# A fused attention and expert-routing kernel: eight pieces for the first layer's weights, halves for the second, and a shorter last add

## What is computed

```python
def _L0_ffn_ref(x, controller, f1, bias, f2):      # x: normalised, (4, 1024, 512)
    grouped = x.reshape(B, g, t, d)                # g = 32 groups of t = 32 tokens
    logits = einsum('bgtd,des->bgtes', grouped, controller) + tie     # e = 32, s = 4
    perm = (logits == max(logits, axis=t))         # each of 128 (e, s) picks one token of a group
    dispatched = einsum('bgtd,bgtes->bgesd', grouped, perm)
    inner = relu(einsum('bgesd,desf->bgesf', dispatched, f1) + bias)  # f = 32
    intermediate = einsum('bgesf,esfd->bgesd', inner, f2)
    return einsum('bgesd,bgtes->bgtd', intermediate, perm)
...
x = x + attention(layernorm(x), ctx)
x = x + ffn(layernorm(x))
```

## Time and profile before

| | before |
|---|---|
| median of 3 runs | 1225.07 us (1223.57 to 1226.09) |
| the profiled execution | 1224.32 us |
| its span from first to last instruction | 1222.6 us |
| mean granted clock of TensorE | 0.979 of full speed |
| TensorE, VectorE, ScalarE, GpSimd busy | 94%, 70%, 49%, 44% of the span |
| DMA | 223.42 MB, mean 183 GB/s |

### The profile page before, as it was taken

One profiled execution on the slowest core, in us unless ns is written; L12 is line 12 of the kernel. 1 busy time (PEld: TensorE's weight loads), 2 busy tenths in 40 slices (PEclk: granted clock), 3 DMA queues, 4 the chain that ended last, 5 costly groups with the idle time before them and its releaser, 6 DMA issues. The chain is left out here.

```text
span 1222.6 us, 28711 instructions
## 1 busy us (share of the span) xinstructions
PE 1145.3 (94%) x11328; PEld 788.3 (64%) x11328; DVE 860.9 (70%) x2200; ACT 599.5 (49%) x1110; POOL 536.2 (44%) x740
## 2 busy tenths in 40 slices
PE   7999999999999999999999999998899997879886
PEld 6787888886555555555555555553578886767664
DVE  7765677763777777777777777774478886755765
ACT  4222222214565566556556655656244443437774
POOL 1000000012777666777766677777566640001344
PEclk9999999999999999999999999999989998989998
DMA  8978877885566444556644456622588874863555
GB/s 288 349 257 295 275 270 262 291 254 157 131 138 139 102 101 105 118 132 139 139 100 103 101 117 136 139 73 69 211 295 265 261 254 125 297 230 87 166 167 166
DMA packets 169733, 223.42 MB, mean 183 GB/s; under 512 B 9728, under 2 KB 97280, under 8 KB 168576
## 3 DMA queue, kind: packets, MB, share of 16 engines
q1 hardware_dynamic: 169600, 221.61, 61.6%
HBM read 143.69 MB, written 77.63 MB: 181 GB/s over the span
## 5 line engine op out<-in xcount | busy, mean ns | idle before, releaser
L1072 ACT ACTIVATE p_t<-p_bank 128x512 f32<-128x512 f32 (+1 forms) x608 | 304.7, 578 | 185.0 <-PE p_bank L1180 182.1
L936 DVE CUSTOM_DVE_ANT_0 tried<-p_bank,ban 128x128 bf16<-128x128 f32 (+3 forms) x512 | 237.2, 485 | 69.9 <-PE p_bank L1159 66.7
L1159 PE MATMUL p_bank<-k_stack,q_stack 96*128 96x512 f32 (+3 forms) x768 | 278.2, 377 | 4.9 <-DVE mx_ab L939 0.8
L1180 PE MATMUL p_bank<-q_stack,k_stack 97*128 97x512 f32 (+3 forms) x768 | 260.0, 359 | 11.2 <-ACT p_t L1072 9.8
L939 DVE TENSOR_REDUCE mx_ab<-p_bank 128x1 f32<-128x512 f32 x256 | 176.1, 688 | 57.2 <-PE p_bank L1159 55.6
L1159 PEld LDWEIGHTS p_bank<-k_stack,q_stack 96*128 96x128 f32 x768 | 144.3, 189 | 103.0 <-issue 39.8
L1180 PEld LDWEIGHTS p_bank<-q_stack,k_stack 97*128 97x128 f32 x768 | 145.6, 191 | 46.4 <-ACT p_t L1072 29.9
L821 POOL TENSOR_SCALAR_AFFINE_SELECT p_t<-p_t 128x128 f32<-128x128 f32 (+2 forms) x288 | 103.7, 362 | 160.2 <-ACT p_t L1072 153.5
L1199 PE MATMUL p_bank<-p_t,v_tile 128*32 128x512 f32 (+3 forms) x1536 | 164.7, 497 | 0.0
L832 POOL TENSOR_TENSOR p_sum<-p_sum,p_t 128x512 f32<-128x512 f32 x128 | 160.1, 1287 | 0.0
L1448 POOL TENSOR_TENSOR kept_o_sum<-kept_o_sum,kept_x_in 128x512 f32<-128x512 f32 x32 | 40.9, 1281 | 179.1 <-ACT kept_o_sum L1476 178.4
(11 more groups left out here) (132 smaller groups left out, 2079.3 us busy)
## 6 DMA issues: line engine op xcount, KB each, us to landing
q_stack<-q_hi SPq DMA_DIRECT2D x64, 256.0 KB, 6.8
k_stack<-k_hi SPq DMA_DIRECT2D x30, 512.0 KB, 9.6
kept_f<-in_f SPq DMA_DIRECT2D x5, 2048.0 KB, 10.7
x_in<-in_x SPq DMA_DIRECT2D x8, 1024.0 KB, 9.9
x_t<-in_x_t SPq DMA_DIRECT2D x8, 1024.0 KB, 9.0
k_hi<-k_hi_s SPq DMA_DIRECT2D x8, 1024.0 KB, 5.9
k_lo<-k_lo_s SPq DMA_DIRECT2D x8, 1024.0 KB, 7.8
v_rows<-v_out SPq DMA_DIRECT2D x8, 1024.0 KB, 7.7
```

The lines of the kernel that those rows point to most:

```text
L936: dve.tensor_tensor_reduce(scrap, got, ban0[:] if i == 0 else ban[:, CH - w:CH], 1.0, -3e38, ALU.add, ALU.max, to[:, col:col + 1]).then_in ...
L1072: act.activation(pt[:, k % SLOTS_P, u * m:(u + 1) * m, 0:w], bank[:, SB + n % SR, 0:m * w].rearrange("p (m w) -> p m w", m=m), ACT.Exp, sc ...
L1159: pe.matmul(bank[:, to, 0:w], qs[it % SLOTS][0:R, i * P // CH, h, i * P % CH:i * P % CH + P], ks[it % SLOTS][0:R, h, t0:t0 + w], start=Tru ...
L1180: mm = pe.matmul(bank[:, SB + n % SR, h % m * w:(h % m + 1) * w], ks[slot][0:R + 1, h, j * P:(j + 1) * P], qs[slot][0:R + 1, sh, h, CH - w ...
```

## The change

It has three parts. (1) The two loads of f1 quarters 0 and 1 (2 MB each, rows of 16 KB) after step 1 become eight loads of 512 KB (rows of 4 KB), after steps 2, 5, 8, ..., 23. The bias stays after step 1. (2) In the second layer the half of the columns becomes the outer loop and the batch the inner one. Each of the four f2 pieces is loaded in two parts: columns 0 to 255 (1 MB, rows of 1 KB) where the whole piece was loaded, columns 256 to 511 after the pick loads. Unit 4, the first of the second half, waits for them. (3) The last two of the 32 sums are no longer copied by ScalarE and added to by GpSimd; VectorE adds x2 to them directly from PSUM.

```diff
+    F1_PARTS = 4
...
             if s == 1:
-                sp.dma_start(keep.f1[:, 0], f1_src[0]).then_inc(f1_early, 16)
-                sp.dma_start(keep.f1[:, 1], f1_src[1]).then_inc(f1_early, 16)
                 sp.dma_start(keep.bias[:], a.bias_col).then_inc(f1_early, 16)
+            if s % 3 == 2 and s // 3 < 2 * F1_PARTS:
+                k, part = divmod(s // 3, F1_PARTS)
+                cols = slice(part * NE * F // F1_PARTS, (part + 1) * NE * F // F1_PARTS)
+                sp.dma_start(keep.f1[:, k, cols], f1_src[k, :, cols]).then_inc(f1_early, 16)
...
-        sp.wait_ge(f1_early, 48)
+        sp.wait_ge(f1_early, 16 + 2 * F1_PARTS * 16)
...
-    SUMS = [(h * CHUNKS + ch, b * 2 + w) for b in range(B) for h in range(HALVES) for ch in range(CHUNKS) for w in range(2)]
+    LAST = 2
+    SUMS = [(h * CHUNKS + ch, b * 2 + w) for h in range(HALVES) for b in range(B) for ch in range(CHUNKS) for w in range(2)]
...
-                    sp.dma_start(f2[i], f2_src[i]).then_inc(f2_in[i], 16)
+                    sp.dma_start(f2[i][:, :, 0:DH], f2_src[i][:, :, 0:DH]).then_inc(f2_in[0][i], 16)
...
                 def store(v):
-                    sp.wait_ge(added, v + 1)
+                    if v < len(SUMS) - LAST:
+                        sp.wait_ge(added, v + 1)
+                    else:
+                        sp.wait_ge(added_last, v - len(SUMS) + LAST + 1)
...
+                for i in range(len(f2)):
+                    sp.dma_start(f2[i][:, :, DH:D], f2_src[i][:, :, DH:D]).then_inc(f2_in[1][i], 16)
...
             def _(pool):
-                for v in range(len(SUMS)):
+                for v in range(len(SUMS) - LAST):
...
-                for w in range(2):
-                    keep_sum(len(SUMS) - 2 + w)
...
+                for v in range(len(SUMS) - LAST, len(SUMS)):
+                    dve.wait_ge(x_in[v % XR], 16 * (v // XR + 1))
+                    dve.wait_ge(stored[v % SR], 16 * (v // SR))
+                    dve.wait_ge(summed, v + 1)
+                    dve.tensor_tensor(o_sum[:, v % SR].rearrange("p n d -> p (n d)"), bank[:, SUM + v % 2],
+                                      x2[:, v % XR].rearrange("p n d -> p (n d)"), ALU.add).then_inc(added_last, 1)
...
-                    b, h, mp, qp = u // HALVES, u % HALVES, pair // 2, pair % 2
+                    b, h, mp, qp = u % B, u // B, pair // 2, pair % 2
                     n = u * PAIRS + pair
+                    if b == 0:
+                        pe.wait_ge(f2_in[h][mp], 16)
                     if u == 0:
-                        pe.wait_ge(f2_in[mp], 16)
                         pe.wait_ge(active, mp * 2 + 2)
```

More of the change, by code:

```diff
@@ L1367, in experts @@
         inner_done = sem("inner_done")
-        f2_in = [sem(f"f2_in{i}") for i in range(len(f2))]
+        f2_in = [[sem(f"f2_in{h}_{i}") for i in range(len(f2))] for h in range(HALVES)]
         pick_in = sem("pick_in")
@@ L1378, in experts @@
         added = sem("added")
+        added_last = sem("added_last")
         xn_src = m.xn.rearrange("(i p) (k d) -> k p i d", p=P, d=P)
```

## The result

The changed kernel takes 1217.59 us (median of 6 runs, 1214.3 to 1218.76), the kernel before 1223.52 in the same comparison. The medians are 5.9 us apart; the ratio of the means (1216.99 and 1223.98) is 0.9943, 95% interval 0.9927 to 0.9959, which is 7.0 us or 0.6% faster, and ratios are of means from here on. In a second comparison it was 0.9941 (0.9918 to 0.9965). The forecast was 1209.5 with a range of 1203 to 1216: the direction was right, and the gain is a little less than half of what was forecast.

What follows compares the result with a forecast made beforehand. TensorE, busy for 94% of the span, was taken as the bound. 10.0 (routing) + 4.0 (expert stage, net) + 1.3 (end) = 15.3 us off 1224.32 gives 1209.0; with the median 0.75 higher, 1209.5, range 1203 to 1216.

Steps and rivals of the forecast that it cites:

- The eight pieces: Routing stage: splitting the two 2 MB f1 loads removes TensorE's hole near 881 to 888, 10.0 us gained.
- upper bound of 15.8 us: Routing stage: the most the pieces could cost, 4.19 MB at 266 GB/s wholly in the tiles' way; 0 was taken.
- (c): Rival, routing stage: the pieces are hidden only in part, costing 3 us of TensorE; 1212.5 us, chance 12%.
- (d): Rival, routing stage: the hole at 881 is the stage's start-up, not the 4 MB, and stays; 1219.5 us, chance 6%.
- (e): Rival, slower: small rows make DMA the bound; routing loses 15.8 us, the halves cost 4; 1233 us, chance 5%.
- The last two sums: End of the kernel: VectorE adds from PSUM instead of ScalarE copying and GpSimd adding, 1.3 us gained.
- The wait for x2: End of the kernel: x2 rows landing after 4.4 us instead of 3.4 would take half the gain, 0.6 to 1.3.
- Stalls of layer one: Expert stage: three large TensorE instruction stalls, 6.70 us in all, shrink to 1.06 each with f2 halved, 3.5 us gained.
- the clock: Expert stage: TensorE's slow clock behind the last stall may go; a third of 3.0 us taken, 1.0 us gained.
- The comparison with the stop at 1038: Layer one: this stop, 1.06 us beside 512-byte rows only, was taken as what each of three large stalls would cost.
- What the second halves add: Start of layer two, 1107 to 1121: second halves of f2 cost 0.5 us, since ScalarE sets the pace; bounds 0 to 4.
- Rival (a): Expert stage: instruction stalls do not depend on what else is queued, and stay; 1214 us, chance 17%.

Runs made afterwards that it cites:

- e5: The changed kernel without loading the second halves of f2; all units use the first halves: 1212.27 us, ratio 0.9903 to the kernel before.
- e1: The changed kernel with each f2 piece loaded whole again (2 MB), no second halves behind the picks: 1213.72 us, ratio 0.9930; again 1212.72, 0.9924.
- e2: The kernel before with the eight f1 pieces alone: 1214.76 us, ratio 0.9943.
- e12: e9 with its four pick loads paced too, two loads on the way at most, picks and f2 together: 1207.65 us, ratio 0.9865 to the kernel before.
- e6: e1 with the expert stage's 2 MB f1 and f2 loads cut into 512 KB, two on the way at most: 1211.58 us, ratio 0.9901.
- e9: e6 with the first f2 piece loaded first, ahead of the raw rows: 1209.96 us, ratio 0.9907; again 1209.70, 0.9887.

## Why the prediction was right and wrong

**The eight pieces, -10.0 us forecast:** right, in the place and in the size. The routing stage went from 151.5 to 141.5 us (141.0 in the shortest). The upper bound of 15.8 us for the pieces' cost falls, and with it rivals (c) and (d) and what (e) says of the routing: in that stage the pieces took nothing from TensorE. What the step did not have is that some of it is lost again afterwards: with the pieces alone the kernel gains 7 us, and layer one takes 3 us more than in two profiles of before, in its last round. Why is open.

**The last two sums, -1.3 us:** right; 1.2 by the profile, too little for the medians. The wait for x2 that would take half of it, named in the prediction, came in four later profiles.

**Stalls of layer one, -3.5 us, and the clock, -1.0 us:** the stops of after sum to 9.85 us against 8.83, and to 7.92 against 9.14 in the second pair, so the term fails as it stands beside before. What it rests on, that fewer bytes beside the gathers mean shorter stops, is seen against the kernels with f1 pieces and whole f2: there the halves take 4.5 us off the stage (95.0 to 90.5 in the means), as much as forecast, but from another starting point, so the agreement is in part luck. Against the profile of before it was 2.6 us. The comparison with the stop at 1038 gave nothing: the stops did not shrink to its 1.06 us but fell at other places, up to 3.15 us long.

**What the second halves add, +0.5 us:** this is the step that failed, with +6.9 us. "I take 0.5 us, since ScalarE sets the pace", and a bound of three blocks of 1.3 us. The stretch of the earlier trace rows was read without its queue: ScalarE led at DMA share 0.02 because blocks came in time there, with one stop of 0.63 us. With 4 MB queued, two blocks came 1.9 and 3.8 us late, TensorE's clock fell to 1.2 GHz after them, and ScalarE waited for TensorE (2.14 and 4.30 us). The two stops sum to 5.65 us, and to 4.19 in the second profile of after, whose start is as long (20.3 us); the rest goes with the clock, 0.75 over the start in both. Without the second halves the start is 13.8 us (e5). The stops that the trace already showed, up to 2.62 us for a block beside 2 to 4 MB, were used for the gain and not for the cost; three of those would have been 8 us. Rival (a), that the stops stay, came true beside the kernel before; the upper 4 us that rival (e) took for the halves was too low by 2.9.

In sum: 10.0 + 1.2 + 2.6 + 0.5 - 6.9 - 0.8 = 6.6 us against 6.4 in the spans (the 0.5 is the rest of layer two, the 0.8 the later start of the routing). And the split as a whole? By the profiles it takes 4.5 us off layer one and puts 6.9 at the start; e1 is ahead of after by 0.0013 and 0.0017 in two comparisons, which the intervals don't separate. No gain of it is seen, and e2 has the whole gain of after (0.9943) from the f1 pieces alone.

The rule of the Trainium skill that was set against the pieces, "DMA: Bandwidth & Descriptors", section Bandwidth (1 MiB or more in a transfer), does not show here: 512 KB pieces cost nothing in the routing stage, and the fastest kernel of the study, e12, moves most of the expert stage's data in loads of 512 KB. The fit by which the prediction estimated 25.6 us is stated on that page for transfers issued by GpSimd; all of these are issued by SyncE. The Trainium skill's rule on a DMA engine's queue rows, same page, section Queues, rings and completion order, would, as the prediction took it, have a block wait for a packet at a time. The trace doesn't agree: 1.85 MB passed before the block that landed at 1104.9, and its packet started 5.15 us behind the block before, where idle DMA engines started one after 1.1 to 2.5. The measurement decides.

## What to carry to other kernels

An engine whose program is long is a user of the DMA engines too: where TensorE stops in the middle of a run with "issue" as the cause, count its instructions against the packets of the instruction queue, look whether such a packet landed just before the stop ended (else it is a wait for data, as in e6), and price every load that is moved beside short matmuls as a wait of the next block. Loads of 512 KB, two on the way at most, gave the fastest kernel here; they cost the issuing engine its lead, and a piece that goes out late is paid in full (3.93 us in e6). A cost that lies hidden in an idle stretch must be priced with the load in it, from the stretches that have one.

## What was not expected of the hardware

- A stop for a block of TensorE's instructions can last 4 us behind queued data (4.29 us in e9), and stops of 2 us are common in layer one with 2 MB loads on the way (2.04 to 2.08 us three times in e1); in the starts of layer two without a load they are 0.63 us or none.
- The length of a row (1 KB or 8 KB) makes no difference to that: 20.7, 20.3 and 20.6 us.
- With the same matmuls and the same bytes in all, layer one and the start of layer two took together from 103.1 us (e9; e12 103.3) to 110.2 us (after), by where the loads stood and how many were on the way.
